# One-core adaLN, path-attention and feed-forward kernel: x loaded ahead of the up matrices, four identity products, head and Q reordered, phi's halves in two gaps

## The chip, the cores and the metric

The kernel runs on one NeuronCore of a Trainium2 chip, in float32 throughout. The metric is the device time of one execution in microseconds. The core has five engines that run side by side, each through its own list of instructions in order: TensorE (PE, with its weight loads as PEld), VectorE (DVE), ScalarE (ACT), GpSimd (POOL) and SyncE (SP). They wait for each other on semaphores only. Matrix products land in PSUM, from which DVE or ACT must carry them away before the bank is used again.

## The reference, cut to what matters

```python
def cond(x, c, ...):            # conditioned bottleneck, D = 256, H = 64
    w_down = down_project * (c @ down_gamma)[:, None, :] + (c @ down_beta)[:, None, :]
    w_up   = up_project   * (c @ up_gamma)[:, None, :]   + (c @ up_beta)[:, None, :]
    return relu(x @ w_down) @ w_up + x
def attn(h, Wp, bp, Wv, Wo):    # 8 heads, 5 path bits
    paths = sigmoid(h @ Wp + bp)
    sim   = cumprod(pq * pk + (1 - pq) * (1 - pk)).sum() / 5     # per pair of tokens, causal
    return (softmax(sim) @ (h @ Wv)) @ Wo
x = x + attn(cond(x))           # B = 4, T = 512
def cond2(x, mu): U = mu @ W_dec + b_dec; return x @ (U @ V)[:-1] + (U @ V)[-1]
def ffn(y): e = argmax(y @ gate_w.T); return y + y @ expert_w[e].T
out = x + ffn(cond2(x))
```

The cumulative product of agreements is computed as an inner product of 32 features per head (the products of the path signs), so that the scores are one small matrix product.

## The kernel before, in words

Everything is transposed, with features on partitions and tokens along the free side. Batches are worked through one after the other. Each batch has six **pairs** of scores and context: p0 and p1 are the first 256 queries of head groups 0 and 1, p2 and p3 the second 256 queries of group 0 in two halves (p2 "opening", p3 closing), p4 and p5 the same for group 1. A pair's scores fill four PSUM banks (`s_ps`), ACT takes their exponential into `prob`, POOL masks the diagonal tile and adds two tiles into `short`, PE forms the context and the sum of the exponentials in `c_ps`, and DVE divides (`rden`, then `ctx_t`). For p2 to p5 DVE adds the tiles first into `tiles` (steps `add`, three instructions for two pairs), and PE multiplies these by ones.

What else has to be done is laid into the **gaps** between scores and context. One Python list, `ORDER`, holds all steps in one order, and every engine goes through it and issues its own part of each step. `PROLOGUE` is its head, `after_scores(b)` gives what stands between the scores of pair p + 1 and the context of pair p, and `after_context(b)` what stands behind that context. The steps that matter here:

- `gdn`: four 128x128 products that broadcast the conditioned down factors (batch 0 alone, then batches 1 to 3); DVE makes `w_dn` from them.
- `gup b`: the same for the up factors of batches 0 and 1 (one 128x512 product each, from `lift_sb`); DVE makes `w_up`. For batches 2 and 3 it goes another way: `ugT` (four products from `lift_sb`), DVE's `w_lift` (which needs `mix_sb`), then `lift b`, two transposes on PE and a copy on ACT.
- `down b` (from `x_t` and `w_dn`, then a relu on ACT into `act_t`), `up b j` (half j of `h_t`, made by DVE), `VL b t` (values and path logits of token tile t, `v_sb` by ACT), `bias`, `tanh` and `feat` (the 32 features, DVE, ACT, DVE), `phi b g` (transposes of the features for head group g, carried out and scaled by ACT or DVE as `scaler` says).
- `U m`, `Uadd`, `ubT`, `WoU`, `G e`, `Q`: the matrices of the second part, made during batch 0. `U` goes through DRAM (`u_scratch`) and back (`u_raw`), and DVE's `Uadd` then makes `u_w`.
- `zT`, `zs`, `zo`, `zoT`, `out`: gate, choice and output of the batch before, in the gaps of the next.

Steps that need a bank of their own take one of `work0` and `work1` in turn (in the head, of six banks, by `EARLY_BANK`); PE waits until the step that held the bank before has been carried away. So a step that is left out, added or moved also changes which step the next one waits for.

SP issues the loads in one fixed order and later the stores. `WARM` is a count of 128x128 products of the identity with itself, which PE runs before anything else and whose results nobody reads.

Of the kernel before, what the change touches and what calls it, by code (L numbers as in the profile page):

```python
# [29 lines left out]
ROWS = 2 * CW  # L30
WARM = 8

# [7 lines left out]
ALL = B * BP  # L40
# [59 lines left out]
def scaler(s):  # L100

    if s[3] == ALL_T:
        return "scalar" if s[2] == 1 or s[1] == 1 else "vector"
    return "scalar" if s[2] == 0 and s[3] == FIRST else "vector"

def features(b, ts):

    return [("bias", b, ts), ("tanh", b, ts)]

PROLOGUE = [("gdn", (0,)), ("gup", 0), ("down", 0), ("gdn", (1, 2, 3)), ("up", 0, 0), ("up", 0, 1), ("gup", 1),
            ("VL", 0, 0), ("VL", 0, 1), *features(0, FIRST), ("feat", 0, FIRST), ("VL", 0, 2), ("VL", 0, 3), ("bias", 0, SECOND),
            ("down", 1), ("phi", 0, 0, FIRST), ("phi", 0, 1, FIRST), ("tanh", 0, SECOND), ("scores", 0),
            ("feat", 0, SECOND), ("phi", 0, 0, SECOND), ("phi", 0, 1, SECOND)]
EARLY_BANK = {("gdn", (0,)): 0, ("gup", 0): 1, ("down", 0): 2, ("gdn", (1, 2, 3)): 3, ("up", 0, 0): 4, ("up", 0, 1): 5,
              ("gup", 1): 0, ("VL", 0, 0): 1, ("VL", 0, 1): 2, ("VL", 0, 2): 4, ("VL", 0, 3): 5, ("down", 1): 0,
              ("phi", 0, 0, FIRST): 1, ("phi", 0, 1, FIRST): 2}

def after_scores(b):
# [3 lines left out]
    if n1 < B:  # L125
        gaps[0] += [("WoU",)] if b == 1 else []
        gaps[0] += [("up", n1, 0), ("up", n1, 1)]
        gaps[3] += [("feat", n1, ALL_T)]
        gaps[4] += [("phi", n1, 0, ALL_T), ("phi", n1, 1, ALL_T)]
    if b == 0:  # L130
        gaps[1] += [("ugT",), ("U", 1)]
        gaps[2] += [("VL", n1, 2), ("VL", n1, 3)]
        gaps[3] += [("lift", 2), ("U", 3)]
        gaps[5] += [("lift", 3), ("Uadd",)]
# [11 lines left out]
def after_context(b):  # L146
# [3 lines left out]
    if b == 0:  # L150
        gaps[0] += [("U", 0)]
        gaps[1] += [("VL", n1, 0), ("VL", n1, 1)]
        gaps[2] += features(n1, ALL_T) + [("U", 2)]
        gaps[4] += [("G", 0), ("ubT",), ("Q",)]
        gaps[5] += [("down", n2), ("G", 1)]
# [6 lines left out]
    if b >= 1 and n1 < B:  # L162
        gaps[0] += [("VL", n1, 0)]
        gaps[1] += [("VL", n1, 2)]
        gaps[2] += features(n1, ALL_T)
        gaps[2] += [("out", prv - 1, 3)] if prv >= 1 else []
    elif prv >= 1:
# [8 lines left out]
for _b in range(B):  # L176
    for _i, (_a, _c) in enumerate(zip(after_scores(_b), after_context(_b))):
# [3 lines left out]
        ORDER += _a  # L181
        if opening(_p):
            ORDER += [("add", _p)]
        ORDER += [("context", _p)]
        ORDER += _c
        if _p + 1 < ALL and long(_p + 1) and not opening(_p + 1):
            ORDER += [("add", _p + 1)]
ORDER += [("zT", B - 1, SECOND), ("out", B - 1, 0), ("zs", B - 1, SECOND), ("zo", B - 1, 1),
          ("out", B - 1, 1), ("zoT", B - 1, 1), ("out", B - 1, 2), ("out", B - 1, 3)]

NO_BANK = ("scores", "context", "add", "bias", "tanh", "feat", "Uadd", "zo")
EARLY = 6
# [11 lines left out]
def build(nc, x_tr, first, lift, vl, mix, bp, W_dec, b_dec, expert_tr, out_tr):  # L204
    with ExitStack() as ctx:
# [131 lines left out]
        def _(sp):  # L337

            sp.dma_start(first_sb[:], first).then_inc(ld_first, 16)
            sp.dma_start(lift_sb[:], lift).then_inc(ld_lift, 16)  # L340
            sp.dma_start(x_t[:, 0], x_tr[0].rearrange("(c p) t -> p c t", p=P)).then_inc(ld_x[0], 16)
# [80 lines left out]
        @block.scalar  # L422
        def _(act):
            for s in ORDER:
                if s[0] == "scores":
# [55 lines left out]
        def _(dve):  # L481
# [23 lines left out]
            for s in ORDER:  # L505
# [11 lines left out]
                elif kind == "ugT":  # L517
                    full(dve, s)
                    nc.vector.tensor_copy(ug_col[:].rearrange("p g b -> p (g b)"), bank(s)[:, 0:2 * DC * B]
                                          ).then_inc(empty(s), 1)  # L520
                    done(dve, s)
                    dve.wait_ge(ld_mix, 16)
# [391 lines left out]
```

## Time and profile before

| | |
|---|---|
| time, median of 3 runs | 148.36 us (147.6 to 149.44) |
| the profiled execution, its own time | 148.48 us |
| its span (first to last instruction) | 146.8 us |
| PE busy | 135.0 us, 92% of the span |
| DVE busy | 99.5 us, 68% |
| ACT busy | 59.3 us, 40% |
| POOL busy | 50.4 us, 34% |
| DMA | 12.62 MB, nearly all of it in the first 31 us |

The span is the part of the execution that the trace covers, and 1.68 us of the execution's time lie around it. A row of the timeline gives start, duration, engine, line, operation, what is written from what, how many records (a float32 product has two), and in brackets how long the engine stood idle before it and what ended that. A row of the chain gives start, duration and what the end of the program was waiting for in that time.

### The profile page before, as it was taken

What the parts mean: (1) busy time and instruction counts of PE and PEld (TensorE: products, weight loads), DVE (VectorE), ACT (ScalarE), POOL (GpSimd) and SP (SyncE); (2) the same over time, 40 slices, a digit from 0 to 9 for tenths busy, and PEclk for the clock granted to TensorE, in tenths of its full rate; (3) what the DMA queues carried; (4) which work ended last, traced back from release to release, by engine and by line L of the source; (5) the groups of instructions that cost most, each with busy time, mean ns of one, the idle gap of its engine ahead of it and who ended that gap; (6) DMA issues with size and microseconds to landing.
All of it is one profiled execution on the core that took longest, in us unless ns stands there. A gap on an engine that the chain in (4) does not pass through costs nothing.

```text
span 146.8 us, 4941 instructions
## 1 busy us (share of the span) xinstructions
PE 135.0 (92%) x2190; PEld 85.6 (58%) x2190; DVE 99.5 (68%) x180; ACT 59.3 (40%) x73; POOL 50.4 (34%) x71
## 2 busy tenths in 40 slices
PE   5688879999989999998899999999899998999992
PEld 5464456654636685665556675657467674657651
DVE  1434557685995866799956859697567967884531
ACT  3011645655664406473531475265316364310010
POOL 7300029006063560660446615602566660300000
PEclk9999999999999999999999999999999999999999
DMA  4899999800022000000110100001101010111212
GB/s 142 277 464 420 384 367 349 308 17 0 2 36 36 4 0 4 0 4 2 40 36 4 38 4 0 26 14 40 36 4 36 4 36 4 38 38 38 71 40 71
DMA packets 7381, 12.62 MB, mean 86 GB/s; under 512 B 1552, under 2 KB 5808, under 8 KB 7232
## 3 DMA queue, kind: packets, MB, share of 16 engines
q1 hardware_dynamic: 7264, 12.26, 23.6%
q8 instruction: 17, 0.28, 0.8%
q0 software_dynamic: 96, 0.05, 0.3%
q14 instruction: 4, 0.03, 0.1%
HBM read 10.09 MB, written 2.22 MB: 84 GB/s over the span
## 4 chain that ended last, share of the span: by engine, by line
PE 58%; DVE 19%; DMA 8%; issue 6%; ACT 2%; POOL 2%; SPq 2%; DVEq 0%; ACTq 0%; POOLq 0%
PE work L666 32%; PE s_ps L666 12%; PE c_ps L666 10%; DMA x_t<-in_x_tr 4%; DVE tiles L606 3%; DMA u_scratch<-u_row 3%; DVE rden L495 2%; DVE tiles L609 2%; ACT prob L434 2%; DMA u_raw<-u_scratch 2%; POOL zo L418 2%; PE work L857 2%; DVE zo L637 1%; PE work L797 1%; DVE feat L656 1%
## 5 line engine op out<-in xcount | busy, mean ns | idle before, releaser
L434 ACT ACTIVATE prob<-s_ps 128x1536 f32<-128x1536 f32 (+1 forms) x24 | 38.2, 1594 | 35.4 <-PE s_ps L666 35.4
L399 POOL TENSOR_SCALAR_AFFINE_SELECT prob<-prob 128x1024 f32<-128x1024 f32 x16 | 18.4, 1150 | 66.3 <-ACT prob L434 66.3
L495 DVE RECIPROCAL rden<-c_ps 128x256 f32<-128x256 f32 x16 | 28.1, 1755 | 6.6 <-PE c_ps L666 6.5
L666 PE MATMUL s_ps<-phi_t 32*128 32x256 f32 (+1 forms) x384 | 24.1, 365 | 0.9 <-DVE phi_t L557 0.6
L666 PEld LDWEIGHTS s_ps<-phi_t 32*128 32x128 f32 x384 | 17.3, 184 | 11.2 <-issue 8.3
L666 PE MATMUL c_ps<-prob,v_sb 128*32 128x256 f32 (+1 forms) x384 | 22.1, 348 | 0.0
L411 POOL TENSOR_TENSOR short<-prob 128x512 f32<-128x512 f32 x15 | 21.0, 1402 | 1.3
L666 PE MATMUL work<-ctx_t,mix_sb 128*32 128x256 f32 x256 | 17.0, 381 | 0.4 <-ACT zo_t L477 0.2
L666 PE MATMUL work<-zo_t,gexp 128*32 128x256 f32 x256 | 16.9, 379 | 0.0
L666 PEld LDWEIGHTS c_ps<-prob,v_sb 128*32 128x32 f32 x384 | 10.7, 109 | 8.8 <-issue 2.8
L666 PE MATMUL work<-w_vl,h_t 128*32 128x296 f32 x208 | 15.1, 415 | 0.4 <-DVE h_t L540 0.4
L644 DVE TENSOR_TENSOR x_t<-work,x_t 128x256 f32<-128x256 f32 x16 | 6.7, 421 | 10.7 <-PE work L666 10.7
L666 PEld LDWEIGHTS work<-zo_t,gexp 128*32 128x32 f32 x256 | 8.6, 110 | 5.2 <-ACT zo_t L477 0.2
L602 DVE TENSOR_TENSOR tiles<-prob 128x1024 f32<-128x1024 f32 x8 | 11.4, 1421 | 0.0
L666 PEld LDWEIGHTS work<-ctx_t,mix_sb 128*32 128x32 f32 x256 | 8.0, 110 | 5.6 <-ACT zo_t L477 0.7
L418 POOL TENSOR_TENSOR zo<-z_nat,pick 128x256 f32<-128x256 f32 x12 | 7.0, 615 | 9.2 <-DVE pick L629 9.2
L606 DVE TENSOR_TENSOR tiles<-tiles,prob 128x512 f32<-128x512 f32 x7 | 8.7, 1236 | 1.5 <-POOL prob L399 1.5
L442 ACT COPY v_sb<-work 128x296 f32<-128x296 f32 x13 | 5.2, 403 | 10.8 <-PE work L666 10.8
L666 PEld LDWEIGHTS work<-w_vl,h_t 128*32 128x32 f32 x208 | 6.1, 109 | 5.2 <-issue 1.2
L477 ACT COPY zo_t<-work 128x512 f32<-128x512 f32 x8 | 4.4, 587 | 9.0 <-PE work L857 9.0
L656 DVE TENSOR_TENSOR feat<-feat,sign 128x64 f32<-128x64 f32 (+4 forms) x20 | 7.2, 359 | 0.7
L496 DVE TENSOR_TENSOR ctx_t<-c_ps,rden 128x256 f32<-128x256 f32 x16 | 6.8, 424 | 0.6
(110 smaller groups left out, 149.3 us busy)
## 6 DMA issues: line engine op xcount, KB each, us to landing
wdec<-in_W_dec SPq DMA_DIRECT2D x1, 3855.0 KB, 17.0
x_t<-in_x_tr SPq DMA_DIRECT2D x4, 512.0 KB, 8.1
ex_t<-in_expert_tr SPq DMA_DIRECT2D x1, 2048.0 KB, 23.2
out_x<-x_t SPq DMA_DIRECT2D x16, 128.0 KB, 1.7
mix_sb<-in_mix SPq DMA_DIRECT2D x1, 904.0 KB, 18.7
lift_sb<-in_lift SPq DMA_DIRECT2D x1, 384.0 KB, 3.0
w_vl<-in_vl SPq DMA_DIRECT2D x1, 296.0 KB, 6.2
first_sb<-in_first SPq DMA_DIRECT2D x1, 144.0 KB, 2.2
```

What stands on the lines that cost most here:

```text
L399: nc.gpsimd.affine_select(out=tri, in_=tri, compare_op=ALU.is_ge, fill=0.0, base=0, pattern=[[0, HG], [0, 2], [1, P]], channel_multiplier= ...
L411: nc.gpsimd.tensor_tensor(short[:, mixes(p) % 2], both[:, :, 0, P:CW], both[:, :, 1, 0:P], ALU.add).then_inc(mixed, 1)
L418: ins = nc.gpsimd.tensor_tensor(zo[:, t], z_nat[:, t:t + 1, :].broadcast_to([P, E, KP]), pick[:, t, :].unsqueeze(2).broadcast_to([P, E, KP ...
L434: nc.scalar.activation(prob[:, p % 2, :, 0:width(p)], s_ps[:, :, 0:width(p)], ACT.Exp).then_inc(exped, 1)
L442: nc.scalar.copy(v_sb[:, b % 2, t, :], bank(s)[:, 0:D + H * DEPTH]).then_inc(empty(s), 1)
L495: link(nc.vector.reciprocal(rden[:], c_ps[m % 2][:, CW:2 * CW]))
L496: nc.vector.tensor_tensor(ctx_t[:, b % 2, g, CW * half:CW * (half + 1)], c_ps[m % 2][:, 0:CW], rden[:], ALU.mult).then_inc(ctx_ready, 1)
L602: nc.vector.tensor_tensor(acc, both[:, :, 0, :], both[:, :, 1, :], ALU.add).then_inc(added, 1)
L606: nc.vector.tensor_tensor(acc[:, :, 0:P], acc[:, :, 0:P], both[:, :, 0, 0:P], ALU.add).then_inc(added, 1)
L644: nc.vector.tensor_tensor(x_t[:, b, c, half], bank(s)[:, 0:CW], x_t[:, b, c, half], ALU.add).then_inc(empty(s), 1)
L656: ins = nc.vector.tensor_tensor(feat[:, rows, n:2 * n], feat[:, rows, 0:n], sign[:, rows, i:i + 1].broadcast_to([P, H * len(ts), n]), ALU. ...
L666: return nc.tensor.matmul(o, w, r, start=start, stop=stop, skip_group_check=True)
```

## The change

- **Loads.** `lift_sb` is no longer the second load of SP's queue. ACT issues it, once the identity is there, as its first instruction. All of SP's loads behind it move up by one, x of batch 0 first.
- **Identity products.** `WARM` is 4 in place of 8.
- **Head.** `gdn (1,2,3)` goes ahead of `gup 0` and `down 0`. `tanh` of the second half goes ahead of `down 1`. `ugT` moves from batch 0's gap 1 to just ahead of the first scores, and `up 1 0` from the gap behind scores 1 to just behind `feat`. `down 1` takes bank 3 instead of 0.
- **Batch 0.** `Q` moves from gap 4 to gap 1, where `ugT` was; DVE's `w_lift` stays there as a step of its own, `wlift`. `lift 3` moves from batch 0's gap 5 to batch 1's gap 2.
- **phi.** The two halves of `phi b+1` no longer stand together in gap 4: the second goes into gap 5. Both are now carried out by ACT for every batch (the first was DVE's for batches 2 and 3).
- **add.** The opening pair's addition is written behind the context of the pair before it, like the closing one's, and no longer ahead of its own context. POOL's additions (`short`) are as before.

```diff
-WARM = 8
+WARM = 4
...
-    if s[3] == ALL_T:
-        return "scalar" if s[2] == 1 or s[1] == 1 else "vector"
-    return "scalar" if s[2] == 0 and s[3] == FIRST else "vector"
+    return "scalar" if s[3] == ALL_T or s[2] == 0 and s[3] == FIRST else "vector"
...
-        gaps[0] += [("up", n1, 0), ("up", n1, 1)]
+        gaps[0] += [("up", n1, 0)] if b else []
+        gaps[0] += [("up", n1, 1)]
         gaps[3] += [("feat", n1, ALL_T)]
-        gaps[4] += [("phi", n1, 0, ALL_T), ("phi", n1, 1, ALL_T)]
+        gaps[4] += [("phi", n1, 0, ALL_T)]
+        gaps[5] += [("phi", n1, 1, ALL_T)]
     if b == 0:
-        gaps[1] += [("ugT",), ("U", 1)]
+        gaps[1] += [("wlift",), ("Q",), ("U", 1)]
...
-        gaps[4] += [("G", 0), ("ubT",), ("Q",)]
+        gaps[4] += [("G", 0), ("ubT",)]
...
+        gaps[2] += [("lift", 3)] if b == 1 else []
...
-        if opening(_p):
-            ORDER += [("add", _p)]
         ORDER += [("context", _p)]
         ORDER += _c
-        if _p + 1 < ALL and long(_p + 1) and not opening(_p + 1):
+        if _p + 1 < ALL and long(_p + 1):
             ORDER += [("add", _p + 1)]
...
             sp.dma_start(first_sb[:], first).then_inc(ld_first, 16)
-            sp.dma_start(lift_sb[:], lift).then_inc(ld_lift, 16)
             sp.dma_start(x_t[:, 0], x_tr[0].rearrange("(c p) t -> p c t", p=P)).then_inc(ld_x[0], 16)
...
         def _(act):
+            act.wait_ge(ident_ready, 1)
+            act.dma_start(lift_sb[:], lift).then_inc(ld_lift, 16)
```

PE at the program's start, before (`first_sb,cond_b` is `gdn`, `lift_sb,cond_b` is `gup`, `x_t,w_dn` is `down`, `act_t,w_up` is `up`, `w_vl,h_t` is `VL`, `ident,feat` is `phi`):

```order
L666 MATMUL c_ps<-ident 128x128 x8
L666 MATMUL work<-first_sb,cond_b 128x128
L666 MATMUL work<-lift_sb,cond_b 128x512
L666 MATMUL s_ps<-x_t,w_dn 32x256 x8
L666 MATMUL s_ps<-first_sb,cond_b 128x128 x3
L666 MATMUL s_ps<-act_t,w_up 128x256 x4
L666 MATMUL work<-lift_sb,cond_b 128x512
```

PE at the same place, after:

```order
L667 MATMUL c_ps<-ident 128x128 x4
L667 MATMUL work<-first_sb,cond_b 128x128
L667 MATMUL s_ps<-first_sb,cond_b 128x128 x3
L667 MATMUL work<-lift_sb,cond_b 128x512
L667 MATMUL s_ps<-x_t,w_dn 32x256 x8
L667 MATMUL s_ps<-act_t,w_up 128x256 x4
L667 MATMUL work<-lift_sb,cond_b 128x512
```

The three products for batches 1 to 3 no longer stand between `down 0` and `up 0`.

PE around the first two scores (`phi_t`), before, up to the first context:

```order
L797 MATMUL s_ps<-ident,feat 128x128 x2
L666 MATMUL s_ps<-phi_t 128x256 x4
L666 MATMUL s_ps<-phi_t 128x128 x4
L797 MATMUL work<-ident,feat 128x128 x4
L666 MATMUL s_ps<-phi_t 128x256 x4
L666 MATMUL s_ps<-phi_t 128x128 x4
L666 MATMUL work<-act_t,w_up 128x256 x4
```

The same after (`first_sb,lift_sb` is `ugT`):

```order
L798 MATMUL s_ps<-ident,feat 128x128 x2
L667 MATMUL work<-first_sb,lift_sb 128x4 x4
L667 MATMUL s_ps<-phi_t 128x256 x4
L667 MATMUL s_ps<-phi_t 128x128 x4
L667 MATMUL work<-act_t,w_up 128x256 x2
L798 MATMUL work<-ident,feat 128x128 x4
L667 MATMUL s_ps<-phi_t 128x256 x4
L667 MATMUL s_ps<-phi_t 128x128 x4
L667 MATMUL work<-act_t,w_up 128x256 x2
```

`ugT` now stands ahead of the first scores, and half of `up 1` ahead of the transposes of the second half.

DVE in batch 1 from the division of p9 to the additions for p11, before:

```order
L495 RECIPROCAL rden<-c_ps 128x256
L496 TENSOR_TENSOR ctx_t<-c_ps,rden 128x256
L644 TENSOR_TENSOR x_t<-work,x_t 128x256
L557 TENSOR_SCALAR phi_t<-work,rootc 128x512
L602 TENSOR_TENSOR tiles<-prob 128x1024
L644 TENSOR_TENSOR x_t<-work,x_t 128x256
```

The same after:

```order
L495 RECIPROCAL rden<-c_ps 128x256
L496 TENSOR_TENSOR ctx_t<-c_ps,rden 128x256
L645 TENSOR_TENSOR x_t<-work,x_t 128x256
L603 TENSOR_TENSOR tiles<-prob 128x1024
L645 TENSOR_TENSOR x_t<-work,x_t 128x256
```

DVE no longer carries out a half of `phi`. PE's part of that step, `ident,feat`, stands as eight transposes ahead of one context before and as four and four ahead of two contexts after.

## Rows read from the trace of the kernel before

**Rows 1.** The page, busy time of each engine with its share of the span

```profile
PE 135.0 (92%) x2190; PEld 85.6 (58%) x2190; DVE 99.5 (68%) x180; ACT 59.3 (40%) x73; POOL 50.4 (34%) x71
```

**Rows 2.** The chain of waits up to the first VL: start, duration, what

```profile
1.72 5.85 DMA x_t<-in_x_tr
...
7.71 1.95 PE s_ps L666 x22
9.68 0.56 DVE w_dn L512
...
10.82 1.22 DVE h_t L540 x2
```

**Rows 3.** The chain of waits, later in batch 0

```profile
39.28 0.57 DVE u_row L572
...
41.12 3.98 DMA u_scratch<-u_row
...
45.54 2.48 DMA u_raw<-u_scratch
...
50.96 0.34 DVE gexp L589
```

**Rows 4.** Timeline of PE, head to batch 0

```profile
5.07 1.02 PE L666 MATMUL work<-lift_sb,cond_b 128*128 128x512 f32 x2
...
8.71 0.94 PE L666 MATMUL s_ps<-first_sb,cond_b 128*128 128x128 f32 x6
...
10.65 1.12 PE L666 MATMUL work<-lift_sb,cond_b 128*128 128x512 f32 x2
12.18 1.20 PE L666 MATMUL work<-w_vl,h_t 128*32 128x296 f32 x16 [0.41 <-DVE h_t L540]
...
18.40 0.94 PE L666 MATMUL s_ps<-phi_t 32*128 32x256 f32 x16 [0.58 <-DVE phi_t L557]
19.97 0.63 PE L797 MATMUL work<-ident,feat 128*128 128x128 f32 x4 [0.64 <-DVE feat L656]
...
25.95 1.05 PE L666 MATMUL work<-first_sb,lift_sb 128*128 128x4 f32 x8
...
44.22 0.61 PE L666 MATMUL work<-mix_sb 128*128 128x8 f32 x4 [0.78 <-DVE gexp L589]
```

**Rows 5.** Timeline of PE, batches 1 and 2

```profile
66.77 0.64 PE L666 MATMUL c_ps<-tiles,ones 128*32 128x256 f32 x8 [0.37 <-DVE tiles L609]
...
71.12 0.66 PE L797 MATMUL work<-ident,feat 128*128 128x128 f32 x4 [0.53 <-DVE x_t L644]
...
106.16 0.64 PE L666 MATMUL c_ps<-tiles,ones 128*32 128x256 f32 x8 [0.62 <-DVE tiles L609]
```

**Rows 6.** DMA issues: queue, count, KB, us from issue to landing

```profile
mix_sb<-in_mix SPq DMA_DIRECT2D x1, 904.0 KB, 18.7
lift_sb<-in_lift SPq DMA_DIRECT2D x1, 384.0 KB, 3.0
```

**Rows 7.** Windows: stretch, length, PE busy (records), PEclk, DMA share, GB/s

```profile
2.00:3.00 1.00, 1.00 (x6) 1.00 0.87 267
...
4.00:5.00 1.00, 1.00 (x9) 1.00 0.96 332
```

**Rows 8.** Weight loads of 128 columns, by tile: ns min/median/max, first and last start

```profile
L666 PEld LDWEIGHTS c_ps<-ident x16: 192/333/338, 1.6 to 4.6; 128*128 128x128 f32 x16
L666 PEld LDWEIGHTS s_ps<-first_sb,cond_b x6: 186/192/192, 8.7 to 9.3; 128*128 128x128 f32 x6
```

**Rows 9.** Timeline of DVE, batches 1 to 3

```profile
74.91 0.68 DVE L606 TENSOR_TENSOR tiles<-tiles,prob 128x512 f32<-128x512 f32 x1
...
100.77 0.75 DVE L557 TENSOR_SCALAR phi_t<-work,rootc 128x512 f32<-128x512 f32 x1 [0.93 <-PE work L797]
...
104.30 1.21 DVE L606 TENSOR_TENSOR tiles<-tiles,prob 128x512 f32<-128x512 f32 x1
...
128.54 1.21 DVE L602 TENSOR_TENSOR tiles<-prob 128x1024 f32<-128x1024 f32 x1
```

More of the change, by code:

```diff
@@ L100, in scaler @@
 def scaler(s):
-    if s[3] == ALL_T:
-        return "scalar" if s[2] == 1 or s[1] == 1 else "vector"
-    return "scalar" if s[2] == 0 and s[3] == FIRST else "vector"
+    return "scalar" if s[3] == ALL_T or s[2] == 0 and s[3] == FIRST else "vector"
 def features(b, ts):
     return [("bias", b, ts), ("tanh", b, ts)]
[L112 to L118, printed above, removed]
+PROLOGUE = [("gdn", (0,)), ("gdn", (1, 2, 3)), ("gup", 0), ("down", 0), ("up", 0, 0), ("up", 0, 1), ("gup", 1),
+            ("VL", 0, 0), ("VL", 0, 1), *features(0, FIRST), ("feat", 0, FIRST), ("VL", 0, 2), ("VL", 0, 3),
+            *features(0, SECOND), ("down", 1), ("phi", 0, 0, FIRST), ("phi", 0, 1, FIRST), ("ugT",), ("scores", 0),
+            ("feat", 0, SECOND), ("up", 1, 0), ("phi", 0, 0, SECOND), ("phi", 0, 1, SECOND)]
+EARLY_BANK = {("gdn", (0,)): 0, ("gdn", (1, 2, 3)): 3, ("gup", 0): 1, ("down", 0): 2, ("up", 0, 0): 4, ("up", 0, 1): 5,
+              ("gup", 1): 0, ("VL", 0, 0): 1, ("VL", 0, 1): 2, ("VL", 0, 2): 4, ("VL", 0, 3): 5, ("down", 1): 3,
+              ("phi", 0, 0, FIRST): 1, ("phi", 0, 1, FIRST): 2, ("ugT",): 0}
 def after_scores(b):
@@ L126, in after_scores @@
         gaps[0] += [("WoU",)] if b == 1 else []
-        gaps[0] += [("up", n1, 0), ("up", n1, 1)]
+        gaps[0] += [("up", n1, 0)] if b else []
+        gaps[0] += [("up", n1, 1)]
         gaps[3] += [("feat", n1, ALL_T)]
-        gaps[4] += [("phi", n1, 0, ALL_T), ("phi", n1, 1, ALL_T)]
+        gaps[4] += [("phi", n1, 0, ALL_T)]
+        gaps[5] += [("phi", n1, 1, ALL_T)]
     if b == 0:
-        gaps[1] += [("ugT",), ("U", 1)]
+        gaps[1] += [("wlift",), ("Q",), ("U", 1)]
         gaps[2] += [("VL", n1, 2), ("VL", n1, 3)]
         gaps[3] += [("lift", 2), ("U", 3)]
-        gaps[5] += [("lift", 3), ("Uadd",)]
+        gaps[5] += [("Uadd",)]
     elif n1 < B:
@@ L189 @@
           ("out", B - 1, 1), ("zoT", B - 1, 1), ("out", B - 1, 2), ("out", B - 1, 3)]
-NO_BANK = ("scores", "context", "add", "bias", "tanh", "feat", "Uadd", "zo")
+NO_BANK = ("scores", "context", "add", "bias", "tanh", "feat", "Uadd", "zo", "wlift")
 EARLY = 6
@@ L520, in _ @@
                                           ).then_inc(empty(s), 1)
-                    done(dve, s)
+                elif kind == "wlift":
+                    done(dve, ("ugT",))
                     dve.wait_ge(ld_mix, 16)
```

## The prediction

> **What bounds the kernel now.** I read the page's busy times first. PE works 92% of the span, no other engine over 68% [rows 1], so a gain can only come out of PE's idle time or out of stretches in which PE is not what the end waits for. The chain of waits shows two such stretches. The first is the head: the end waits 5.85 us for x of batch 0, which SP issues third, and PE's `down 0` starts only at 7.71; behind it stand products and then DVE's `w_dn` before `h_t` [rows 2]. The second is late in batch 0: from DVE's copy of `u_row` at 39.28 the chain runs through DRAM and back (3.98 and 2.48 us of waiting) to DVE's `gexp` at 50.96, for whose bank PE's `up 2 0` waits [rows 3]. The timeline of PE, read for its brackets, then gives the idle pieces that the change touches: 0.58, 0.64 and 0.78 in batch 0 [rows 4], 0.37, 0.53 and 0.62 later [rows 5]. Elsewhere PE's products stand without a gap, so a step moved from one gap to another there is worth nothing by itself.
>
> **Part 1, the loads.** The up matrices took 3.0 us from issue to landing as the second load [rows 6]. In the new order x is issued where they were, at about 1.26, and ACT issues them once the identity is there, at about 1.55 (PE's first product on the identity began at 1.6 [rows 8]). PE needs both: `gup 0` stands ahead of `down 0` and takes 1.02 [rows 4]. The DMA engines are full at that time (share 0.87 and 0.96, 267 and 332 GB/s [rows 7]). The first load, x and the up matrices are 144 + 512 + 384 = 1040 KB, whoever issues them: 267 until 3.0, some 300 until 4.0, 332 until 5.0, and the last 140 by 5.4. With a little for the landing I let both be there at 5.7, PE do `gup 0` until 6.8, and `down 0` start at 6.8: **0.9 us gained**. The ends: the up matrices 3.0 us after issue, at 4.55, and x no later than `gup 0` ends; PE is then free of `gdn` at about 5.1, and `down 0` starts at 6.1 (1.6 gained); or both take the 5.85 us that x took, the up matrices land at 7.4 and `down 0` starts at 8.4 (0.7 lost). I take the middle because the rate in the windows is a measured one and the bytes ahead of `down 0` are the same.
>
> **Part 2, `gdn` ahead.** Its products held PE from 8.71, for about 0.87 us, between `down 0` and `up 0`, and DVE's `w_dn` held `h_t` from 9.68 to 10.82 [rows 2, 4]. Both now lie before the up matrices land, where PE and DVE have nothing else. What is late next is PE itself: `up 0`, then `gup 1`, which ended at 10.65 + 1.12 = 11.77, 0.41 before `VL` began at 12.18 [rows 4]. So the first `VL` comes 0.41 earlier plus what `up 0` comes earlier, which is between nothing and 0.87; the relu on ACT between them needs some of it, and I take 0.35. **0.75 us gained**, ends 0.41 and 1.28.
>
> **Part 3, four identity products fewer.** They run beside the first load; without them `gdn 0` starts at about 3.5 instead of 4.84, and nothing waits for it. Nothing gained, as long as the clock rises as before (a rival, below). With parts 1 and 2 the head gives 1.65. The loads behind it leave room: `mix_sb`, the latest that is needed soon, lands at 3.69 + 18.7 = 22.4 [rows 6], and `wlift` and `Q` want it at about 24.
>
> **Part 4, around the first scores.** `ugT` costs PE 1.05 [rows 4] and now stands in an idle piece of 0.58, so scores 0 come 0.45 later. DVE's small copy of its result stands ahead of `feat`, which was ready to start at 18.4, so `feat` comes about 0.7 later, and the last transposes now also wait for a bank that `h_t` empties behind `feat`. I put scores 1 at 0.7 later. Against that half of `up 1` (0.55) now lies in the idle 0.64, and in gap 1 `ugT`'s 1.05 is replaced by `Q`'s 0.5 (0.61 with its tail [rows 4]). 0.55 + 1.05 - 0.5 - 0.7 = 0.4; masks and the fuller DVE take some, so **0.3 gained**, ends 0 and 0.6.
>
> **Part 5, `Q` and `lift 3` leave the end of batch 0.** PE loses the wait of 0.78 for `gexp`, `Q`'s 0.5 and `lift 3`'s 0.4, and gains a half of `phi` only in place. But the end of that batch is set by the chain of [rows 3], which begins with an exponential and a mask at 31 us, contains neither `Q` nor a transpose, and ends in the bank that `up 2 0` waits for in both kernels. So PE only arrives earlier and waits longer there: **0 gained**, upper end 1.3.
>
> **Part 6, `lift 3` in batch 1.** About 0.4 of PE work ahead of the wait of 0.37 at 66.77, which it covers [rows 5]: 0.05 lost, ends 0.4 lost and 0.
>
> **Part 7, `phi` in two gaps.** In batch 1 the second half waited 0.53 for a bank [rows 5]; now the bank was emptied long before. The 0.5 us of its transposes moves behind the next scores and so ahead of the product on `tiles`. That product waits for DVE, whose last two additions start when `out` is carried away, so by then they and not PE are last: of 0.53 + 0.09 I take 0.4. In batch 2 the product on `tiles` waited 0.62 [rows 5], behind an addition that took 1.21 where the same one took 0.68 in batch 1, because POOL's addition ran beside it [rows 9]. DVE's copy of `phi` (0.75 [rows 9]) goes to ACT, which is 40% busy, so DVE's `tiles` addition comes earlier and no longer holds POOL up, and the moved transposes fill the rest: 0.6. **1.0 gained**, ends 0.3 and 1.2. The stretch before the last batch's closing waits is bound by POOL and isn't touched.
>
> **Part 8, the opening addition.** It changes DVE's order in the last batch alone: 1.21 us [rows 9] go ahead of `zs`, and the last product on `tiles` no longer waits about 0.1 for them. `zoT` then finds `zo` ready with little to spare. **0.1 gained**, ends 0.5 lost and 0.15.
>
> **Sum.** 0.9 + 0.75 + 0.3 + 0 - 0.05 + 1.0 + 0.1 = 3.0 us. From the profiled execution's 148.48 that is 145.5; the median of the runs is 0.12 lower, so I say **145.4 us**, 2% under 148.36. About 2% is what a measurement of this kernel can tell from no change, so the forecast lies on that border (145.4).
>
> **Rivals.**
> - *The loads don't come earlier.* x and the up matrices share the DMA engines, and `down 0` starts where it did. For it speaks that x took 5.85 us although the 1040 KB ahead of and with it would do by 5.4, so some part of it is not rate. Only part 2 and the rest are left, 2.1 us: 146.4. Chance 0.22.
> - *More than forecast.* The up matrices land at 4.6 (0.7 more), and the end of batch 0 or the scores give back another 0.5: 144.2. For it speaks that the up matrices took 3.0 us in the same crowd, against it the chain through DRAM. Chance 0.17.
> - *The clock rises later.* The first products ran slowly: their weight loads took 333 ns in the median and 192 at the end, where the same load took 192 at 8.7 us [rows 8]. That is the level of 1.2 GHz and then that of 2.4, although the window says 1.00 [rows 7]; the rise came after some 3 us of unbroken products, which now have a hole ahead of `gdn` and one ahead of `gup`. If it comes with `down 0`, `gup 0` costs its 1.02 again, and half of `down 0` some 0.5: 146.9. Chance 0.13.
> - *Slower than before.* The same place, but the rise waits for products without holes, and the head has none before the first `VL`. Then `gup 0`, `down 0`, `up 0` and `gup 1` cost themselves again (1.02 + 1.0 + 1.1 + 1.12 = 4.2), `VL` too: 3.0 gained, 4.2 and more lost, 149.6 and up. It decides from a rise at about 11 us on, where three of the four are done slowly. Against it: in the kernel before PE was idle from about 6.1 to 7.7 and the products behind were fast. Chance 0.07. The Trainium skill, "TensorE: Matmul & The Clock Gate", under "What's actually happening", says that the throttled state is the default and that activity releases it; that is what would make this happen, and the first and last loads on the identity agree.
>
> **How the numbers follow.** 0.41 for the forecast with a range of its own of 144.8 to 146.1, the rest as given. The low end takes in the better case with its bounds (143.8), the high end the late clock (147.4); what lies outside is most of the slower case and little else. Faster by over 2%, that is under 145.4: all of the better case and seven tenths of the forecast's, 0.46. Slower by over 2%: the slower case where the clock comes well behind the first `VL`, 0.06. Within 2%: 0.48.
>
> **What would show it.** In the profile after: `down 0` at 6.8 (right between 6.1 and 7.5); the first `VL` 3.7 behind it instead of 4.5; weight loads on the identity all near 333 ns, and those of `gup 0` at 192 (if not, the clock); scores 0 about 0.45 later behind the first transposes; a wait of over a microsecond ahead of `up 2 0`, which replaces the 0.78; no wait of `phi` in batch 1, and the one at the `tiles` product of batch 2 under 0.2. The prediction is wrong if the up matrices land behind x by more than `gup 0` can take, if the chain through DRAM shortens, or if DVE and POOL, which hold each other up where they meet, meet more often in the new order.

## The result, and the profile after

The changed kernel took 150.12 us (median of 4 executions, 149.65 to 150.38) beside 147.98 us of the kernel before (4 executions, 147.58 to 149.44). The ratio is 1.0111, with a 95% interval of 1.0059 to 1.0164. The change made the kernel slower, by less than 2%. The forecast was 145.4 us with a range up to 147.4, so the time lies above the range. The profiled execution took 149.65 us, with a span of 147.9.

A ratio here leaves out executions that lie over 1.5% above the fastest of the same kernel, so where such late ones are the subject (the changed kernel again, the old one with four identity products), their counts are given.

The page of the kernel after, busy times:

```profile
PE 137.1 (93%) x2182; PEld 86.0 (58%) x2182; DVE 97.9 (66%) x178; ACT 60.3 (41%) x75; POOL 49.1 (33%) x71
```

PE has 8 records fewer than in [rows 1] and is busy 2.1 us longer. Fewer records take longer. The timeline of PE after the change shows where (`ident` are the identity products):

```profile
1.58 2.08 PE L667 MATMUL c_ps<-ident 128*128 128x128 f32 x8 [1.58 <-POOL ident L371]
3.63 0.79 PE L667 MATMUL work<-first_sb,cond_b 128*128 128x128 f32 x2
4.21 1.49 PE L667 MATMUL s_ps<-first_sb,cond_b 128*128 128x128 f32 x6
7.54 2.08 PE L667 MATMUL work<-lift_sb,cond_b 128*128 128x512 f32 x2 [1.84 <-DMA lift_sb<-in_lift]
9.55 1.93 PE L667 MATMUL s_ps<-x_t,w_dn 128*32 128x256 f32 x16
12.08 1.14 PE L667 MATMUL s_ps<-act_t,w_up 64*128 64x256 f32 x8 [0.59 <-ACT act_t L438]
13.15 1.12 PE L667 MATMUL work<-lift_sb,cond_b 128*128 128x512 f32 x2
14.65 1.21 PE L667 MATMUL work<-w_vl,h_t 128*32 128x296 f32 x16 [0.37 <-DVE h_t L541]
...
19.64 0.44 PE L798 MATMUL work<-ident,feat 128*128 128x128 f32 x2
...
21.88 1.13 PE L667 MATMUL work<-act_t,w_up 64*128 64x256 f32 x4
...
23.79 0.44 PE L798 MATMUL work<-ident,feat 128*128 128x128 f32 x2 [0.41 <-DVE h_t L541]
24.16 0.94 PE L667 MATMUL s_ps<-phi_t 32*128 32x256 f32 x16
25.02 1.13 PE L667 MATMUL work<-act_t,w_up 64*128 64x256 f32 x4
```

Two rows of the same timeline before the change, `down 0` and `up 0`:

```profile
7.71 1.07 PE L666 MATMUL s_ps<-x_t,w_dn 128*32 128x256 f32 x16 [1.62 <-DMA x_t<-in_x_tr]
...
9.58 1.14 PE L666 MATMUL s_ps<-act_t,w_up 64*128 64x256 f32 x8
```

Read three things. `gup 0` waits 1.84 us for the up matrices and then takes 2.08 where the same two records took 1.02 [rows 4]; `gup 1`, the same work again, takes 1.12 at 13.15. `down 0` takes 1.93 instead of 1.07. So TensorE ran at its 1.2 GHz level until past `down 0`, and at 2.4 from `up 0` on. `down 0` begins at 9.55, not at 6.8, and the first `VL` at 14.65, 2.47 later than before. And half of `up 1` costs 1.13 with four records, as much as `up 0` costs with eight.

The chain of waits after the change, its head and the end of batch 0:

```profile
1.56 5.94 DMA lift_sb<-in_lift
...
43.90 3.97 DMA u_scratch<-u_row
...
48.31 2.32 DMA u_raw<-u_scratch
```

The DMA issues after the change, the up matrices and w_vl (queue, count, KB, us from issue to landing):

```profile
lift_sb<-in_lift ACTq DMA_DIRECT2D x1, 384.0 KB, 5.9
w_vl<-in_vl SPq DMA_DIRECT2D x1, 296.0 KB, 6.0
```

The end no longer waits for x but for the up matrices, 5.94 us instead of the 3.0 of [rows 6]. The second chain, through DRAM, stands as in [rows 3]. Later in the kernel the timeline of PE shows what was gained:

```profile
47.02 0.66 PE L798 MATMUL work<-ident,feat 128*128 128x128 f32 x4 [0.80 <-DVE gexp L590]
...
54.07 1.46 PE L667 MATMUL work<-act_t,w_up 64*128 64x256 f32 x8 [0.87 <-DVE gexp L590]
...
69.43 0.64 PE L667 MATMUL c_ps<-tiles,ones 128*32 128x256 f32 x8
...
77.01 0.66 PE L798 MATMUL work<-ident,feat 128*128 128x128 f32 x4
...
107.63 0.61 PE L667 MATMUL c_ps<-tiles,ones 128*32 128x256 f32 x8
...
130.95 0.61 PE L667 MATMUL c_ps<-tiles,ones 128*32 128x256 f32 x8
```

The brackets of [rows 5] (0.37, 0.53 and 0.62) are gone; the 0.78 of [rows 4] has moved from `Q` to `phi`, and `up 2 0` waits 0.87 where it waited 0.17. With the places of the same steps in the two timelines, the difference between the spans (1.1 us) splits like this, where minus is a gain:

| stretch | before | after | difference | forecast |
|---|---|---|---|---|
| start to first `VL` | 12.18 | 14.65 | +2.47 | -1.65 |
| from there to `VL` of batch 1 | 16.67 | 16.99 | +0.32 | -0.3 |
| from there to `up 2 0` | 22.50 | 22.43 | -0.07 | 0 |
| `up 2 0` to the last product | 92.87 | 91.26 | -1.61 | -1.05 |

Three of the four rows differ from the forecast by more than 0.5 us, but only the head by as much as 4.1.

### The profile page after: what moved, and what is told of

Same layout as the page of the kernel before. It is cut to its first block, busy times and chain, and to the rows that moved or that the text cites. A ratio compares the mean times of both kernels' runs of the same rounds, so it can differ in the third digit from the quotient of the medians.

```text
span 147.9 us, 4925 instructions
## 1 busy us (share of the span) xinstructions
PE 137.1 (93%) x2182; PEld 86.0 (58%) x2182; DVE 97.9 (66%) x178; ACT 60.3 (41%) x75; POOL 49.1 (33%) x71
## 4 chain that ended last, share of the span: by engine, by line
PE 72%; DVE 10%; DMA 8%; issue 4%; POOL 3%; SPq 1%; ACT 1%; POOLq 0%; DVEq 0%; ACTq 0%
PE work L667 36%; PE s_ps L667 16%; PE c_ps L667 14%; DMA lift_sb<-in_lift 4%; DMA u_scratch<-u_row 3%; PE work L858 2%; PE work L798 2%; DVE tiles L607 2%; POOL zo L416 2%; DMA u_raw<-u_scratch 2%; DVE h_t L541 1%; DVE rden L495 1%; DVE tiles L610 1%; PE work L850 1%; POOL prob L397 1%
## 5 line engine op out<-in xcount | busy, mean ns | idle before, releaser
L409 POOL TENSOR_TENSOR short<-prob 128x512 f32<-128x512 f32 x15 | 20.1, 1338 | 1.3
L603 DVE TENSOR_TENSOR tiles<-prob 128x1024 f32<-128x1024 f32 x8 | 10.5, 1308 | 0.0
L607 DVE TENSOR_TENSOR tiles<-tiles,prob 128x512 f32<-128x512 f32 x7 | 9.4, 1339 | 1.5 <-POOL prob L397 1.5
```

Source lines behind the costliest of these rows:

```text
L409: nc.gpsimd.tensor_tensor(short[:, mixes(p) % 2], both[:, :, 0, P:CW], both[:, :, 1, 0:P], ALU.add).then_inc(mixed, 1)
L603: nc.vector.tensor_tensor(acc, both[:, :, 0, :], both[:, :, 1, :], ALU.add).then_inc(added, 1)
L607: nc.vector.tensor_tensor(acc[:, :, 0:P], acc[:, :, 0:P], both[:, :, 0, 0:P], ALU.add).then_inc(added, 1)
```

## The experiments

Two theories stood at first. By the first, the low clock behind the hole is the loss, and both come from the load of the up matrices together with the four identity products. The rival: the late landing alone costs the time (PE waits), and the clock has no part in it. Each expectation is quoted, then the measurement. "Before" is the kernel before on the same chip, with a median of 148.3 or 148.4 us each time.

**More identity products, load left on ACT.**

```
-WARM = 4
+WARM = 8        (then 14)
```

> The changed kernel with eight identity products again. Theory (the clock): in the changed kernel gup 0 took 2.08 and down 0 1.93 us where they took 1.02 and 1.07 before, because TensorE was still at the slow level until about 11.4 us. With eight products the rise should come as early as before; gup 0 still waits for the up matrices until 7.5, then 1.0 each, down 0 at 8.6, first VL at about 12.4, and the whole 2.2 us shorter than the changed kernel: ratio to before about 0.996. Rival (the load alone): the rise does not depend on the four products, gup 0 stays at 2.08, and the time is that of the changed kernel, ratio 1.011.

Measured: 0.9987 (0.9958 to 1.0015), median 148.03 of 10 executions. Timeline of PE:

```profile
5.59 1.35 PE L667 MATMUL s_ps<-first_sb,cond_b 128*128 128x128 f32 x6
8.00 1.13 PE L667 MATMUL work<-lift_sb,cond_b 128*128 128x512 f32 x2 [1.06 <-DMA lift_sb<-in_lift]
9.05 1.07 PE L667 MATMUL s_ps<-x_t,w_dn 128*32 128x256 f32 x16
...
13.29 1.21 PE L667 MATMUL work<-w_vl,h_t 128*32 128x296 f32 x16 [0.37 <-DVE h_t L541]
```

The up matrices land even later than in the changed kernel (8.0 against 7.5), and yet the kernel is 2 us faster, because `gup 0` and `down 0` take 1.13 and 1.07 instead of 2.08 and 1.93. The rival falls. Two of the 10 executions lay at 149.8 and 149.9, with a granted clock of 0.988 over the whole, which the kernel before shows as well (last section).

> The changed kernel with fourteen identity products, so that TensorE is busy nearly until the up matrices land at about 7.5. Theory (it is the hole between gdn and gup 0, with the up matrices late, that keeps the clock down or lets it fall): the rise comes early in every execution, gup 0 and down 0 take 1.0 each from 7.5 on, the first VL at 12.7, and no execution lies over 149.5; ratio to before 0.992 to 1.000. Rival (the rise is a matter of chance, whatever stands ahead): some of them at 150 and more, as with four and eight products.

Measured: 0.9991 (0.9959 to 1.0023), 148.01; no execution of 10 above 148.8. PE stands ready at 8.65 there and the first `VL` comes at 13.84; in the trace that is 0.55 later than with eight, and the medians don't differ.

**The load back on SP, second, as before.**

```
+            sp.dma_start(lift_sb[:], lift).then_inc(ld_lift, 16)   # behind first_sb
...
-            act.wait_ge(ident_ready, 1)
-            act.dma_start(lift_sb[:], lift).then_inc(ld_lift, 16)
```

> The changed kernel with the up matrices loaded by SP as the second load again, four identity products. Theory (the clock): gup 0 can start at about 5.2 instead of 7.5, but the products up to the rise stay slow; x lands at 7.6 as before, down 0 starts at 7.7, and if the rise is still at 11 us down 0 takes 1.93 and the first VL comes at 12.5 to 13; ratio to before about 0.995. Rival (the load alone): with the load back the whole loss is gone and the first VL comes at 11.4, 3.2 us shorter than the changed kernel, ratio 0.989.

> a_liftsp once more (up matrices second on SP, four identity products, all else as changed), for more executions. Theory (with the up matrices early there is no long hole ahead of gup 0, and four products do as well as eight): no more than 3 in 10 above 148.5, ratio 0.985 to 0.991. Rival (four products are too few in themselves): half of the executions 2 us and more above the rest.

> The changed kernel with both the load and the eight identity products as before, so that only the moved steps are left of the change. Both theories: first VL at 11.4 (12.18 less the 0.75 of gdn taken off the path), some 0.3 lost or gained around the first scores, and the 1.6 us that the changed kernel gained behind batch 0: 2.0 to 2.7 us under before, ratio 0.982 to 0.987.

Measured: four identity products 0.9885 (0.9826 to 0.9944) and again, on another chip, 0.9902 (0.987 to 0.9933), medians 146.51 and 146.47; eight products 0.9889 (0.9847 to 0.9931), 146.87. None of these 23 executions is above 147.5. The two timelines of PE, first with four, then with eight:

```profile
5.23 1.02 PE L666 MATMUL work<-lift_sb,cond_b 128*128 128x512 f32 x2
7.55 1.07 PE L666 MATMUL s_ps<-x_t,w_dn 128*32 128x256 f32 x16 [1.30 <-DMA x_t<-in_x_tr]
...
11.78 1.20 PE L666 MATMUL work<-w_vl,h_t 128*32 128x296 f32 x16 [0.38 <-DVE h_t L540]
```

```profile
5.85 1.02 PE L666 MATMUL work<-lift_sb,cond_b 128*128 128x512 f32 x2
6.83 1.07 PE L666 MATMUL s_ps<-x_t,w_dn 128*32 128x256 f32 x16
...
8.48 1.14 PE L666 MATMUL s_ps<-act_t,w_up 64*128 64x256 f32 x8 [0.58 <-ACT act_t L437]
...
11.05 1.20 PE L666 MATMUL work<-w_vl,h_t 128*32 128x296 f32 x16 [0.38 <-DVE h_t L540]
```

The load alone turns 1.1% slower into 1.1% faster: 3.6 us between the medians. Here the expectation by the clock was wrong and its rival right: with four products and the early load `down 0` takes 1.07 and not 1.93, so the clock rises early, and four products are enough. In the changed kernel both losses, the wait and the slow products, go with the load. With eight, the gain stays behind what was expected (0.982 to 0.987); part of it is missing around the first scores, below. In the traces eight products are 0.7 us ahead at the first `VL`, in the medians 0.4 us behind, so differences under about half a microsecond are not to be read from medians here.

**The old kernel with one of the two edits.**

```
-WARM = 8                                                    (first kernel)
+WARM = 4
```

```
-            sp.dma_start(lift_sb[:], lift).then_inc(ld_lift, 16)    (second kernel)
...
+            act.wait_ge(ident_ready, 1)
+            act.dma_start(lift_sb[:], lift).then_inc(ld_lift, 16)
```

> The kernel before with four identity products and nothing else. Theory (the clock): the hole between the identity products and gdn and a late rise make down 0, gdn, up 0 slow, 1 to 2.5 us lost, ratio 1.007 to 1.017. Rival (no effect of the products): the rise comes as before, ratio 1.000.

> The kernel before with the new loads alone: the up matrices issued by ACT, x ahead of them, eight identity products. Theory (the up matrices land at about 7.5, since they share the DMA engines with x and w_vl): gup 0 at 7.6, down 0 at 8.6 instead of 7.7, 0.9 to 1.3 us lost, ratio 1.006 to 1.010. Rival, the prediction's sum: both land at 5.7 and down 0 starts at 6.8, ratio 0.994.

Measured, four products in the old kernel: six of 10 executions at 147.3 to 148.6 (0.9967, 0.9925 to 1.0009) and four at 149.9 to 151.2, so neither of the two expectations holds for all of them. The profiled one was a late one, with `gup 0` at 4.21 taking 2.05 and `down 0` 1.93. The load alone, with eight products: 1.026 (1.0172 to 1.0348), 151.84, all four between 150.7 and 152.5. That is more than the whole change lost, and beyond what I had expected of it by either theory. Timeline of PE of that one:

```profile
5.17 0.63 PE L667 MATMUL work<-first_sb,cond_b 128*128 128x128 f32 x2
7.22 2.07 PE L667 MATMUL work<-lift_sb,cond_b 128*128 128x512 f32 x2 [1.42 <-DMA lift_sb<-in_lift]
9.22 1.76 PE L667 MATMUL s_ps<-x_t,w_dn 128*32 128x256 f32 x16
```

The last weight loads of 128 columns ahead of that hole took 333 ns, so the clock had not risen when it opened. Eight identity products do not protect if the hole follows at 5.8; in the kernel above, with `gdn (1,2,3)` still to do, it followed at 6.9 and did no harm.

**The changed kernel again, and its hole filled.**

> The changed kernel once more, unaltered, for the spread of its executions. In the runs so far the executions of the kernel before fell into two groups, 147.4 to 149.0 and 149.7 to 150.7, and all four of the changed kernel lay at 149.7 to 150.4. Theory (the clock rises late in nearly every execution of the changed kernel): at least 8 in 10 above 149.5. Rival (chance): a good part of them at 147 to 148.

Measured: 10 executions with a median of 151.35: eight between 150.6 and 151.9, one of 149.4, one of 147.85. On the same chip the kernel before has 148.28, so this is 2.1% between the medians. (The ratio, 1.0031, 0.9965 to 1.0097, rests on the last two executions alone and says nothing of the others.) The timeline of PE of its profiled execution:

```profile
8.03 1.12 PE L667 MATMUL work<-lift_sb,cond_b 128*128 128x512 f32 x2 [2.46 <-DMA lift_sb<-in_lift]
9.09 1.75 PE L667 MATMUL s_ps<-x_t,w_dn 128*32 128x256 f32 x16
11.41 2.09 PE L667 MATMUL s_ps<-act_t,w_up 64*128 64x256 f32 x8 [0.57 <-ACT act_t L438]
13.43 2.08 PE L667 MATMUL work<-lift_sb,cond_b 128*128 128x512 f32 x2
```

And a window of it (stretch, length, busy PE, PEld, DVE, ACT and POOL, then PEclk, DMA share, GB/s):

```profile
12.00:16.00 4.00, 4.00 (x18) 1.50 (x18) 1.68 (x3) 0.00 (x0) 0.00 (x0) 0.50 0.95 409
```

Another course, of about the same cost. The last weight loads ahead of the hole of 2.46 us still took 333 ns, yet `gup 0` behind it took 1.12, so the full level came within the hole. Then the clock fell early in `down 0` (granted 0.83 from 9.0 to 9.5, 0.50 from there) and stayed at half (0.50) until about 16. A granted clock of 0.976 or 0.977 over the whole, as in this execution, stands at five of the fourteen executions of the changed kernel; seven have 1.0 and took 149.65 to 151.9, like the one whose rows stand first.

```
+                        for _ in range(6):                  # between gdn and gup 0
+                            mm(c_ps[0][:, 0:P], ident[:], ident[:])
```

> The changed kernel with four identity products at the start, as it has, and six more between gdn and gup 0, where TensorE otherwise waits for the up matrices. Theory (the hole is the cause): gup 0 still waits until the up matrices land, at 7.2 to 8.0, but it and down 0 take 1.0 each in nearly every execution, and at most 1 in 10 lies above 149.5; ratio to before 0.990 to 1.000. Rival (it is the number of products ahead of the first matrix work): most executions at 150 and more, as in the changed kernel.

Measured: 0.999 (0.9962 to 1.0017), 147.97; all 10 executions between 147.2 and 148.5. Four products at the start and the late load are kept; only the hole is smaller:

```profile
5.36 2.16 PE L667 MATMUL c_ps<-ident 128*128 128x128 f32 x12
8.04 1.12 PE L667 MATMUL work<-lift_sb,cond_b 128*128 128x512 f32 x2 [0.51 <-DMA lift_sb<-in_lift]
9.10 1.07 PE L667 MATMUL s_ps<-x_t,w_dn 128*32 128x256 f32 x16
```

So the cause is that PE has nothing to do ahead of `gup 0`, neither the count at the start nor the queue as such. The six products shorten the hole and let PE's work last longer at the same time, and no run tells these two apart. Length alone can't be it: with the load on SP and four products a hole of 1.30 and of 1.54 us opened at 6.2 in the two traces, and none of 13 executions was late.

**The halves of `up 1`.** "Together" takes them side by side in gap 0 again, in the changed kernel with the load second on SP and eight products; "split" is the old kernel with nothing but the halves apart.

```
-            ("feat", 0, SECOND), ("up", 1, 0), ("phi", 0, 0, SECOND), ("phi", 0, 1, SECOND)]
+            ("feat", 0, SECOND), ("phi", 0, 0, SECOND), ("phi", 0, 1, SECOND)]
...
-        gaps[0] += [("up", n1, 0)] if b else []
-        gaps[0] += [("up", n1, 1)]
+        gaps[0] += [("up", n1, 0), ("up", n1, 1)]
```

> The changed kernel with the old loads and eight identity products, and the two halves of up 1 together behind scores 1 again. Theory (the two halves of up run at the same time when they stand together, 8 records in 1.14 us, and cost 1.1 each when they stand apart): 0.7 to 1.1 us under the same kernel with them apart, ratio 0.981 to 0.984 to before. Rival (each half costs 0.55 wherever it stands, and filled an idle piece): the same or slower, ratio 0.989 to 0.992.

> The kernel before with the two halves of up 1 apart and nothing else. Theory (they no longer run at the same time): 0.6 to 1.0 us lost around the first scores, ratio 1.004 to 1.007. Rival (half of it fills the idle 0.64): 0.3 to 0.5 gained, ratio 0.997.

> c_up_together once more, on the same chip as the next one. Both theories: 146.0 to 146.6 in the executions with a granted clock of 1.0, and at most 3 in 10 with 0.988.

Measured: together 0.9898 (0.9822 to 0.9974), 146.49, and again 0.9885 (0.9834 to 0.9935), 146.25; split 1.0012 (0.9975 to 1.0048), 148.43. Timeline of PE, together, then split:

```profile
20.24 0.63 PE L796 MATMUL work<-ident,feat 128*128 128x128 f32 x4 [0.86 <-DVE feat L655]
...
21.82 1.14 PE L665 MATMUL work<-act_t,w_up 64*128 64x256 f32 x8
```

```profile
18.04 1.13 PE L667 MATMUL work<-act_t,w_up 64*128 64x256 f32 x4
...
19.95 0.44 PE L798 MATMUL work<-ident,feat 128*128 128x128 f32 x2 [0.42 <-DVE h_t L541]
...
21.19 1.13 PE L667 MATMUL work<-act_t,w_up 64*128 64x256 f32 x4
```

Eight records together take 1.14, four alone 1.13. From the first transposes to `VL` of batch 1 it is 11.38 us together (17.07 to 28.45) against 12.01 split in the changed kernel, and 12.31 split (15.94 to 28.25) against 11.68 together in the old one: 0.63 both times. The times can't confirm so little: the interval around the split kernel's 1.0012 includes both 1 and the 1.0043 that 0.63 us would be, and the two ratios of "together" lie at the rival's 0.989 to 0.992, above the 0.981 to 0.984 expected. What speaks against the rival is the traces alone: a half costs 1.13, not 0.55.

**The order of the two loads on SP.** The kernel "together" with x ahead of the up matrices, both on SP.

> As c_up_together (old loads, eight identity products, the halves of up together), but SP issues x second and the up matrices third, both ahead of w_vl. Theory (what made the up matrices late was w_vl, which shares the DMA engines with them when ACT issues them): x at 4.6, the up matrices at 6.1 to 6.5, down 0 at 7.2 to 7.6, no later than with the up matrices second (6.8 to 7.9 in the profiles so far), and the same time, ratio 0.985 to 0.991. Rival (the up matrices must be first because gup 0 stands ahead of down 0): down 0 0.7 later, and the hole ahead of gup 0 makes the clock late in some executions, ratio 0.993 and more.

Measured: 0.9882 (0.9834 to 0.9929), 146.65. x landed at about 4.7 and the up matrices at about 6.0, `gup 0` began at 6.87 and the first `VL` came at 12.14, against 12.09 with the other order. `down 0` began at 7.90, later than the 7.2 to 7.6 expected, and in the other order at 7.86 and 8.06. Given to SP in front of w_vl, the two orders are equal.

**`phi` back in one gap**, with DVE's share of carrying it out, in the kernel "together".

```
-        gaps[4] += [("phi", n1, 0, ALL_T)]
-        gaps[5] += [("phi", n1, 1, ALL_T)]
+        gaps[4] += [("phi", n1, 0, ALL_T), ("phi", n1, 1, ALL_T)]
```

> As c_up_together, with both halves of phi in gap 4 again and the first one carried out by DVE for batches 2 and 3, as before. Theory (this part of the change gained 0.60 and 0.65 us in batches 1 and 2 in the trace of the changed kernel): 1.0 to 1.4 us slower than c_up_together, ratio 0.997 to 0.999 to before. Rival (the gain came from the opening additions, which stay): 0.3 slower at most, ratio 0.991.

Measured: 0.9953 (0.9905 to 1.0002), 147.39. From `up 2 0` to the product on `tiles` in the last batch it takes 70.45 us (52.13 to 122.58), and 69.42 with `phi` in two gaps (50.89 to 120.31): **1.03 us**. The ratio lies between the theory's range and the rival's 0.991. On the same chip the executions at a granted clock of 0.998 or more had medians of 146.79 (6 of them) and, with `phi` in two gaps and the other load order, 145.88 (7): 0.9 us, beside the 1.03 of the traces.

**`Q` and `lift 3` back to the end of batch 0**, in the kernel "together"; run twice. Both were moved at once, so what follows holds for the two together.

```
-        gaps[1] += [("wlift",), ("Q",), ("U", 1)]
+        gaps[1] += [("wlift",), ("U", 1)]
...
-        gaps[4] += [("G", 0), ("ubT",)]
+        gaps[4] += [("G", 0), ("ubT",), ("Q",)]
...
-        gaps[5] += [("Uadd",)]
+        gaps[5] += [("lift", 3), ("Uadd",)]        (and no lift 3 in batch 1)
```

> As c_up_together, with Q in gap 4 of batch 0 and lift 3 in its gap 5 again. Theory (the end of batch 0 is set by the chain through DRAM, so that PE only waits elsewhere): the 0.5 of Q leaves gap 1, so the chain begins 0.5 earlier, and the end of batch 0 loses less than that; 0.2 to 0.6 us faster than c_up_together, ratio 0.985 to 0.988. Rival (the wait of 0.78 for gexp costs time when it comes back): 0.5 to 0.8 slower, ratio 0.993 to 0.995.

> c_q_lift_back once more. Theory (with Q in gap 4 TensorE idles 1.55 us for gexp, and the granted clock falls there): the executions with a clock of 1.0 are 0.2 to 0.6 us under those of c_again, but more than half have 0.988 and lie 1.5 us higher, so that the median is 0.5 to 1.2 us above that of c_again. Rival (the 7 in 10 with 0.988 seen before were chance): as many with 0.988 as in c_again, and the median lower.

Measured: 0.9919 (0.9861 to 0.9976), 147.7, and 0.9971 (0.9934 to 1.0007), 147.55. Of 20 executions six had a granted clock of 1.0 and took 145.55 to 146.97; fourteen had 0.988 and took 147.24 to 148.5. Of eight of the kernel "together" one had 0.988. Timeline of PE in the profiled execution of the first run, which had 0.988:

```profile
42.83 0.61 PE L664 MATMUL work<-mix_sb 128*128 128x8 f32 x4 [1.55 <-DVE gexp L587]
43.37 1.58 PE L664 MATMUL s_ps<-phi_t 32*128 32x256 f32 x16
```

A window of the same execution, columns as above:

```profile
43.00:47.00 4.00, 4.00 (x34) 3.06 (x38) 2.38 (x7) 2.00 (x3) 1.04 (x2) 0.57 0.24 31
```

`Q` waits 1.55 us for a bank, and in this execution the clock fell behind that wait, so that scores that take 0.94 took 1.58. In the second run's trace the same wait of 1.55 stands and the clock stayed. While the clock holds, the new place of `Q` gains nothing that these runs show: the executions at 1.0 have medians of 145.92 with `Q` back and 146.43 without, and 146.48 and 146.25 on the one chip that has both. It pays by the share of executions that keep the clock. That the wait makes the clock fall is inferred from this share and from the one trace in which the place of the fall can be seen.

## Why the prediction was wrong, step by step

**The step that failed is Part 1 together with the condition of Part 3.** Part 1 let the up matrices land at 5.7, from a rate and a sum of bytes; they landed at 7.5, just past the end of 7.4 that the text gave for x's 5.85 us. x landed at about 4.7, 3.5 us from its issue and earlier than assumed. So the sign that the text itself had named came true: the up matrices landed 2.8 us behind x, more than `gup 0` can take. What Part 1 left out is what the up matrices meet on the way. As second load on SP they took 3.0 us; issued by ACT they took 5.9, and 5.6 to 6.4 in the other traces. w_vl, which SP issued 0.15 later, landed at 7.7, 0.2 behind them, which fits two loads that share the engines; as a load of SP ahead of w_vl, but behind x, the up matrices took 4.2 and landed at 6.0. How much of the 2.9 us each of SP's other loads took, no run shows. The Trainium skill, "DMA: Bandwidth & Descriptors", under "Issuing engines are not separate DMA queues", says that loads of different issuing engines interleave; the trace agrees (7.5 and 7.7), and the prediction had quoted it without taking its price. That alone is 1.8 us at `gup 0` against the forecast.

Part 3's zero was given "as long as the clock rises as before". The rival "slower than before" named the place and the mechanism, at a chance of 0.07, and of its 4.2 us the 1.92 of `gup 0` and `down 0` came (1.06 and 0.86). The reason against it was that the old kernel had a hole from 6.1 to 7.7 and fast products behind it; but there the clock had risen before the hole. In the changed kernel the hole opened at 5.7, before the clock had risen, and in the old kernel with the load on ACT at 5.8, with eight identity products and a clock that had not risen either. What the runs put in place of the argument: with the hole filled 147.97, with eight or fourteen products 148.0, with an early load 146.5; with the load edit alone in the old kernel 151.84. Together with the hole itself this is why the head lost 2.47 us. The Trainium skill, "TensorE: Matmul & The Clock Gate", under "What's actually happening", has the throttled state as the default that activity releases; the traces agree in so far as both fillings of the hole restore the full level.

**Part 2 was mis-sized**: 0.75 was forecast, 0.41 to 1.28. From `down 0` to the first `VL` it was 4.47 us before and 4.22 in the kernel with the early load and eight products, so 0.25, under the low end. Two covers were misread. `gdn`'s 0.87 on PE had hidden the relu on ACT, and that wait is now 0.58; `up 0` comes only 0.22 earlier behind `down 0`. And `w_dn` had held `h_t` for almost nothing: in DVE's timeline `h_t` began 0.09 us behind the start of `gup 1` before (10.74 and 10.65) and 0.06 behind it after (13.21 and 13.15). What is late is `h_t` itself, 1.29 us on DVE against the 1.12 of `gup 1`, so of the wait of 0.41 ahead of `VL` 0.38 stay.

**Part 4 had the wrong sign.** Scores 1 came 0.78 later behind the transposes, as forecast (0.7). But half of `up 1` was counted at 0.55, half of 1.1. It costs 1.06, from its start to that of the next product. The two halves read different halves of the partitions (rows 0 to 63 and 64 to 127 of `act_t` and `w_up`), and together they run side by side in the array; the Trainium skill, "TensorE: Matmul & The Clock Gate", under "Part 3: Packing small matmuls — row/col tiling", describes such products on different row groups as concurrent, and the trace agrees (8 records 1.14, 4 records 1.13). So 0.32 was lost where 0.3 should be gained; keeping the halves together is worth 0.63 in two pairs of traces.

**Part 5 was right about the chain** (22.43 against 22.50 to `up 2 0`, which waits 0.87) and blind to what the idle pieces do to the clock; in the kernels with an early load the new places of `Q` and `lift 3` are worth 1.1 to 1.3 us between medians on the same chip (147.7 to 146.65, with the other load order, and 147.55 to 146.25), by the share of executions that keep the clock.

**Parts 6 and 7 had the right mechanism and nearly the right size.** The forecast was 0.95 together, with an upper end of 1.2. The measured gain was 0.60 from `up 2 0` to the last product on `tiles` of batch 1 (24.90 to 24.30) and 0.65 from there to the one of batch 2 (29.91 to 29.26), 1.25 in all, and `phi`'s two gaps alone 1.03. **Part 8** gained 0.30 instead of 0.1 in the last batch (7.76 to 7.46 between the two products on `tiles`); it was not tried alone. All of this is one pair of traces, apart from the 1.03.

The **upper end** of the range took in a late clock that cost 1.5 us, but no case in which a late load and a late clock come together, though the first makes the second. Treated as one case it would have been 3.0 - 1.8 - 1.9 = -0.7, that is 149.2 from the profiled 148.48; Parts 2 and 4 as measured add 1.1, the later batches take 0.6 off: 149.7, and the profiled execution took 149.65. Three figures of the text don't follow from it: without the gain of Part 1 the time is 146.3 (148.36 - 2.1), not 146.4; seven tenths of the forecast can't lie under 145.4 when 145.4 is the forecast; and the slower rival, priced from 149.6 up, 0.8% above before, can hardly give nearly all of its 0.07 to "slower by over 2%".

**Left open.** Why the clock rises before, in or behind the same hole from one execution to the next; why the old kernel with four identity products was late in 4 of 10 executions and the changed one with the early load in none of 13, though PE is busy until 6.2 or 6.3 in both; whether `Q` or `lift 3` keeps the clock; and whether joining the halves of `up` pays in the median. It leaves a wait of 0.86 for `feat`, and of 28 executions of the kernels with joined halves and `Q` in gap 1 eight had a clock of 0.987 or 0.988, of 53 of the changed kernel with split halves and an early load or a smaller hole two. The trace of the kernel with `phi` in one gap shows the fall behind that wait. ACT's carrying of `phi` and the two gaps were not tried apart.

The best versions are the change with the up matrices second on SP (0.9885 and 0.9902 with four identity products, 0.9889 with eight), the same with the halves joined and eight identity products (0.9898 and 0.9885), and that with x ahead of the up matrices (0.9882). They are about 1.1% faster than the kernel before and can't be told apart; the change as it was is 1.1% slower, and 2.1% in its ten further executions.

## What to carry to other kernels

Before a load changes queue, list what will share the DMA engines with it from issue to landing, and ask what PE waits for first; here a load that was issued 0.3 us later landed 3.2 us later. Where PE may run out of work before its clock has risen, count the products behind the hole at half clock too (here a hole of 1.84 us and 1.92 us of slower products), and treat the load and the clock as one case. Products that use different halves of the rows belong next to each other: count them as one when they are together, and as a whole each when they are apart.

## What the runs showed of the hardware that was not expected

The clock fell in the middle of the kernel too, behind PE waits of only 1.55 us and 0.85 us in the two traces that show it. The executions with such a clock, fourteen of 20 and four of 10, took 1.8 and 2.3 us longer in the median than the others of the same kernel. A window of the second, from the kernel with `phi` in one gap:

```profile
20.00:24.00 4.00, 3.94 (x28) 2.89 (x28) 0.91 (x2) 2.03 (x2) 2.36 (x2) 0.57 1.07 358
```

The kernel before does it as well: 17 of its 99 executions on four chips had a clock of 0.988 or 0.989, and took 149.41 to 150.7 us; none of these was profiled, so where their clock falls is not known. And the low level at the start of a program isn't in the granted clock of the first windows: it reads 1.00 while the same load of 128 columns takes 333 ns instead of 192 [rows 7, 8]. There only the durations tell.
